# A linear-attention and expert kernel: queries projected transposed, two chunks and half of the heads at a time

## What is computed

```python
q = _heads(x @ wq.T)
k = _heads(x @ wk.T)
v = _heads(x @ wv.T)
# _phi(x, omega):
proj = jnp.einsum('bhnd,md->bhnm', x, omega)
norm = 0.5 * jnp.sum(x * x, axis=-1, keepdims=True)
return jnp.exp(proj - norm) / math.sqrt(M)
# then, with phi_q and phi_k:
kv_cumsum = jnp.cumsum(jnp.einsum('bhnm,bhnd->bhnmd', phi_k, v), axis=2)
out = jnp.einsum('bhnm,bhnmd->bhnd', phi_q, kv_cumsum)
z = 1.0 / (jnp.einsum('bhnm,bhnm->bhn', phi_q, jnp.cumsum(phi_k, axis=2)) + 1e-06)
```

## Time and profile before

| | |
|---|---|
| median of 3 runs | 728.42 us (727.18 to 729.02) |
| the profiled execution: its time, its span | 727.18 us, 725.1 us |
| granted TensorE clock, mean | 0.992 |
| busy share: PE, PEld, DVE, ACT, POOL | 96%, 83%, 74%, 53%, 46% |

### The profile page before, as it was taken

The page is one execution under the profiler, slowest core; times in us unless marked ns, Lnnn a source line. Parts: engine busy times, 40 slices in busy tenths (PEclk is TensorE's granted clock), DMA queues, the critical chain, the costliest instruction groups (busy, mean ns, idle before and its releaser), DMA issues. The chain is left out here.

```text
span 725.1 us, 27349 instructions
## 1 busy us (share of the span) xinstructions
PE 697.4 (96%) x11452; PEld 604.1 (83%) x11452; DVE 536.0 (74%) x1685; ACT 387.6 (53%) x740; POOL 335.6 (46%) x625
## 2 busy tenths in 40 slices
PE   8999999999999999999999999999999789999956
PEld 8788888888888888888888888888887779999942
DVE  6687888878878887888878878888775456565416
ACT  5755566665656665666656566665552144544310
POOL 3002545555544445454545554545447306556550
PEclk9999999999999999999999999999999999999989
DMA  9974000000000000000000000000000154553128
GB/s 252 362 268 178 11 9 11 10 9 11 14 15 10 11 10 11 10 10 11 9 11 11 14 14 9 11 11 11 10 11 14 49 177 130 168 173 113 51 82 304
DMA packets 32705, 47.25 MB, mean 65 GB/s; under 512 B 4132, under 2 KB 20168, under 8 KB 32584
## 3 DMA queue, kind: packets, MB, share of 16 engines
q1 hardware_dynamic: 23296, 32.62, 13.4%
q0 software_dynamic: 4096, 8.42, 3.6%
q10 hardware_dynamic: 5192, 4.47, 1.9%
HBM read 22.21 MB, written 23.36 MB: 63 GB/s over the span
## 5 line engine op out<-in xcount | busy, mean ns | idle before, releaser
L1297 POOL DMA_INDIRECT y_rows<-y_sb,row_id x64 | 62.8, 982 | 66.0 <-DVE y_sb L1442 49.9
L1108 POOL DMA_INDIRECT dispatched<-h_cur,slot x64 | 67.3, 1051 | 17.8 <-issue 16.1
L1376 ACT ACTIVATE hidden<-bank,b_col 128x512 f32<-128x512 f32 x64 | 43.3, 689 | 58.2 <-PE bank L1348 57.8
L632 ACT ACTIVATE phi_k<-expo_k 128x1024 f32<-128x1024 f32 x32 | 33.9, 1058 | 74.5 <-DVE expo_k L768 70.7
L648 ACT COPY v_sb<-bank 128x512 f32<-128x512 f32 x64 | 37.6, 587 | 62.1 <-PE bank L279 58.7
L527 PEld LDWEIGHTS bank<-woT,attT 128*128 128x128 f32 x512 | 61.9, 192 | 3.2 <-ACT attT L738 0.6
L859 DVE TENSOR_TENSOR scores<-bank,within 128x512 f32<-128x512 f32 x64 | 41.2, 686 | 31.2 <-PE bank L310 31.2
L527 PE MATMUL bank<-woT,attT 128*128 128x128 f32 x512 | 62.4, 275 | 0.4 <-ACT attT L738 0.4
L1317 PE MATMUL bank<-w_sb,hidden 128*128 128x128 f32 x512 | 59.7, 275 | 0.8 <-issue 0.8
L137 POOL TENSOR_TENSOR rs<-var,power 128x1 f32<-128x1 f32 x64 | 37.1, 579 | 49.8 <-DVE var L132 49.5
L1317 PEld LDWEIGHTS bank<-w_sb,hidden 128*128 128x128 f32 x512 | 58.3, 192 | 1.2 <-issue 1.2
(11 more groups left out here) (243 smaller groups left out, 2037.9 us busy)
## 6 DMA issues: line engine op xcount, KB each, us to landing
dispatched<-blank SPq DMA_DIRECT2D x16, 524.0 KB, 3.1
region<-dispatched SPq DMA_DIRECT2D x30, 262.0 KB, 2.9
y_rows<-blank SPq DMA_DIRECT2D x8, 512.0 KB, 3.9
w_nat<-in_L_ffn_w_dram SPq DMA_DIRECT2D x8, 256.0 KB, 3.7
y_got<-y_rows SPq DMA_DIRECT2D x8, 256.0 KB, 6.8
y_got<-y_rows ACTq DMA_DIRECT2D x8, 256.0 KB, 7.4
out_dram<-x_sb SPq DMA_DIRECT2D x8, 256.0 KB, 3.7
w_sb<-in_L_ffn_w_dram ACTq DMA_DIRECT2D x6, 256.0 KB, 2.8
```

Source lines behind the costliest of these rows:

```text
L1108: pool.indirect_dma_start(out=dispatched[:, :], in_=h2_cur[par][:], in_offset=None, out_offset=bass.IndirectOffsetOnAxis(ap=slot[par][:, k ...
L1297: pool.indirect_dma_start(out=y_rows[:, :], out_offset=bass.IndirectOffsetOnAxis(ap=row_id[par][:, t:t + 1].bitcast(U32), axis=0), in_=y_s ...
L1376: act.activation(hidden[par][:, k, :], psum[2 + k][:], ACT.Gelu, bias=b1_col[:, bass.ds(e * KH + k, 1)]).then_inc(sem(f"hid{k}_out"), 1)
```

## The change

Of the queries, step c now handles unit n = c + 2. A unit is half of the heads (even or odd n) for the two chunks of a pair. `project_qT` holds 128 columns of `wq` as the stationary operand and streams the 256 tokens of the pair, so that the queries come out transposed: 12 matmuls of 128x256 for a unit. ACT copies them to `qT` (`qT_out`), DVE squares them whole (`square_q`), and `exponent_qT` makes the exponent on PE: omega times q plus a matrix of -0.5 times the squares, 16 f32 matmuls with a 64x64 stationary operand and 256 streamed columns, on the quarters of the array in turn. ACT takes the exponential straight out of PSUM into `phiT_q` (`exps_q`). The weights of pq, the projections q and pq of the old form, the transposes tq and their copies, and DVE's sum and exponents for q are gone. Both feature scales are now one factor on the keys' side. `h` is made four chunks ahead instead of two, with three pairs of buffers. The banks are shared out anew (k and pk in banks 2 and 3, wo behind attT0, rank in bank 7, the first state increment in its own turn), k, v and pk stand next to each other, `wo` before the rank, POOL's scatter ahead of the second normalisation, DVE's `find_places` behind `upd`, and the opening is ordered anew: it now holds two units of queries, the first transposes of the keys, and two more chunks of `h`. The indentation below is cut by 16 columns.

```diff
+h_hi = [tsb(f"h_hi{i}", [P, 2, 2, P], F32R) for i in range(3)]
...
+qT = tsb("qT", [P, HD])
+qT_square = tsb("qT_square", [P, HD])
+omT = tsb("omT", [P, M])
+minus_half = tsb("minus_half", [P, M])
+phiT_q = [tsb(f"phiT_q{i}", [P, NP, 2 * P]) for i in range(2)]
...
-X_PIECES = ((0, 1), (1, 2), (3, 9), (12, 10), (22, 10))
+X_PIECES = ((0, 1), (1, 3), (4, 8), (12, 10), (22, 10))
...
-TURNS = {0: ["q0", "k0", "v0", "pq0", "pk0"], 1: ["q1", "k1", "v1", "pq1", "pk1"],
-         2: ["tk0", "tk1", "a0", "attT0"], 3: ["tq0", "tq1", "a1", "attT1", "rank"],
+TURNS = {0: ["q0", "v0", "pq0"], 1: ["q1", "v1", "pq1"],
+         2: ["tk0", "k0", "pk0", "a0", "attT0", "wo"], 3: ["tk1", "k1", "pk1", "a1", "attT1"],
          4: ["o0", "o2", "h2T", "lg"], 5: ["o1", "o3"],
-         6: ["late0", "hT", "late1"], 7: ["early0", "early1", "wo"]}
+         6: ["hT", "late0", "late1"], 7: ["early0", "early1", "rank"]}
 BANK = {k: b for b, ks in TURNS.items() for k in ks}
-BEFORE = {k: ks[i - 1] for ks in TURNS.values() for i, k in enumerate(ks)}
...
+        def project_qT(n):
+            first = 2 * (n % 2)
+            pair = n // 2
+            hi, lo = h_hi[pair % 3][:, :, 0, :], h_lo[pair % 3][:, :, 0:P]
+            pe.wait_ge(sem("h_split"), 2 * pair + 2)
+            if n == 1:
+                pe.wait_ge(sem("wT_split"), len(WEIGHTS))
+            for side in range(2):
+                if n == 0:
+                    pe.wait_ge(sem(f"v{side}_out"), 1)
+                elif n >= 2:
+                    pe.wait_ge(sem(f"pq{side}_out"), 1 if n == 2 else n)
+                for i in range(2):
+                    o = q_bank(side, n)[:, i * 2 * P:(i + 1) * 2 * P].rearrange("p (c t) -> p c t", t=P)
+                    cols = slice(side * 512 + (first + i) * P, side * 512 + (first + i + 1) * P)
+                    pe.matmul(o, wT_hi["q"][:, cols], hi, start=True, stop=False)
+                    pe.matmul(o, wT_lo["q"][:, cols], hi, start=False, stop=False)
+                    mm = pe.matmul(o, wT_hi["q"][:, cols], lo, start=False, stop=True)
+                mm.then_inc(sem(f"q{side}_in"), 1)
+        def exponent_qT(n, c):
+            if c >= 0:
+                pe.wait_ge(sem("v1_out"), c + 2)
...
+                pe.wait_ge(sem("q_squared"), n + 1)
+            for i in range(2):
+                for w, of in ((omT, queries_of(n)), (minus_half, squares_of(n))):
+                    for side in range(2):
+                        for r in range(2):
+                            cols = slice(side * 512 + i * 2 * P, side * 512 + (i + 1) * 2 * P)
+                            mm = pe.matmul(q_bank(r, n)[half_rows(side), i * 2 * P:(i + 1) * 2 * P],
+                                           w[half_rows(r), :], of[half_rows(r), cols],
+                                           start=(w is omT), stop=(w is minus_half), skip_group_check=True)
+                            if i == 1 and w is minus_half and side == 1:
+                                mm.then_inc(sem(f"pq{r}_in"), 1)
...
+            if c < 0:
                 pe.wait_ge(sem("wT_split"), SPLIT[w] + 2)
+                if w == "k":
+                    pe.wait_ge(sem("h_split"), 1)
+                elif w == "v":
+                    pe.wait_ge(sem(f"k{half}_out"), 1)
+                else:
+                    pe.wait_ge(sem("woT_ready"), 2)
+            elif w == "k":
+                pe.wait_ge(sem(f"tk{half}_out"), c + 1)
+            elif w == "v":
+                pe.wait_ge(sem(f"q{half}_out"), min(c + 3, NCH))
+                if c + 2 >= NCH:
+                    pe.wait_ge(sem(f"pq{half}_out"), NCH)
+            else:
+                pe.wait_ge(sem(f"k{half}_out"), c + 2)
+            bank = psum[BANK[kind]] if w == "v" or w == "pk" else k_bank(half, c)
             cols = slice(half * 512, (half + 1) * 512)
...
+        def features_T(half, c, par):
+            if c >= 2:
+                pe.wait_ge(sem("attT1_out" if half else "wo_out"), c - 1)
+            elif c == 1:
+                pe.wait_ge(sem(f"a{half}_out"), 1)
+            pe.wait_ge(sem("phi_k_ready"), c + 1)
...
+                    pe.wait_ge(sem("pk1_out"), c + 2)
...
-            weights(5)
-            pe.wait_ge(sem("h_split"), 1)
-            project("q0", -1, 0)
-            project("q1", -1, 0)
+            for n in range(2, 6):
+                weights(n)
+            project("k0", -1)
+            project("k1", -1)
+            first_T(1)
+            closing_weights()
+            pe.wait_ge(sem("small_used"), 3)
             weights(6)
             weights(7)
+            project("v0", -1)
+            project("v1", -1)
             modulation(1)
-            project("k0", -1, 0)
-            project("k1", -1, 0)
-            project("v0", -1, 0)
-            project("v1", -1, 0)
-            weights(8)
-            weights(9)
-            first_T(1)
-            project("pq0", -1, 0)
-            project("pq1", -1, 0)
-            closing_weights()
+            first_T(2)
+            project("pk0", -1)
+            project("pk1", -1)
+            first_T(3)
+            project_qT(0)
+            project_qT(1)
             modulation(2)
             modulation(3)
-            project("pk0", -1, 0)
-            project("pk1", -1, 0)
-            bias_T()
+            exponent_qT(0, -1)
+            features_T(1, 0, 0)
+            features_T(0, 0, 0)
+            exponent_qT(1, -1)
...
+            if c:
+                pe.wait_ge(sem("gain1_out"), c)
+            else:
+                pe.wait_ge(sem("mod_used"), 4)
+            if live(c, 4):
+                pe.wait_ge(sem("xn_ready"), c + 5)
+                pe.transpose(psum[BANK["hT"]][:, 0:P], xn[par][:], ident[:]).then_inc(sem("hT_in"), 1)
+            if c:
+                features_T(1, c, par)
+                features_T(0, c, par)
+            if live(c, 2):
+                project_qT(c + 2)
             if front:
-                pe.wait_ge(sem("h_split"), c + 2)
-                project("q0", c, nxt)
-                project("q1", c, nxt)
-            features_T("tq0", c, par)
-            features_T("tk0", c, par)
-            if front:
-                project("k0", c, nxt)
-                project("k1", c, nxt)
-            features_T("tq1", c, par)
-            features_T("tk1", c, par)
+                project("k0", c)
+                project("k1", c)
+                project("v0", c)
+                project("v1", c)
+                project("pk0", c)
+                project("pk1", c)
             if tail:
                 attend_state(1, c - 1, nxt, (j - 1) % CPB)
             state_gain(0, c, par, j)
             if tail:
                 attend(1, c - 1, nxt, (j - 1) % CPB)
-            if front:
-                project("v0", c, nxt)
-                project("v1", c, nxt)
             score(0, c, par)
             score(1, c, par)
+            if live(c, 2):
+                exponent_qT(c + 2, c)
             if last:
                 routing_T(c, par)
-            if live(c, 2):
-                pe.wait_ge(sem("gain0_out"), c + 1)
-                pe.wait_ge(sem("xn_ready"), c + 3)
-                pe.transpose(psum[BANK["hT"]][:, 0:P], xn[par][:], ident[:]).then_inc(sem("hT_in"), 1)
-            if front:
-                project("pq0", c, nxt)
-                project("pq1", c, nxt)
+            if tail:
+                attended_T(0, c)
             if last:
                 routing_logits(c)
             if tail:
-                attended_T(0, c)
                 attended_T(1, c)
-            if c == 0:
-                pe.wait_ge(sem("woT_ready"), 2)
             attend_state(0, c, par, j)
             state_gain(1, c, par, j)
             attend(0, c, par, j)
+            if tail:
+                add_heads(c)
             if last:
                 routing_rank(c)
-            if front:
-                project("pk0", c, nxt)
-                project("pk1", c, nxt)
-            if tail:
-                add_heads(c)
...
+        def qT_out(n):
+            if n >= 2:
+                act.wait_ge(sem("pq1_in"), n)
+            for side in range(2):
+                act.wait_ge(sem(f"q{side}_in"), n + 1)
+                act.copy(queries_of(n)[:, side * 512:(side + 1) * 512], q_bank(side, n)[:]).then_inc(sem(f"q{side}_out"), 1)
...
+        def exps_q(n):
+            pairs = phiT_q[n // 2 % 2][:, n % 2 * 4:n % 2 * 4 + 4, :].rearrange("p (s r) t -> p r s t", r=2)
+            for r in range(2):
+                act.wait_ge(sem(f"pq{r}_in"), n + 1)
+                act.activation(pairs[:, r], q_bank(r, n)[:].rearrange("p (s t) -> p s t", t=2 * P),
+                               ACT.Exp).then_inc(sem(f"pq{r}_out"), 1)
...
+        def square_q(n):
+            dve.wait_ge(sem("q1_out"), n + 1)
+            dve.tensor_tensor(squares_of(n), queries_of(n), queries_of(n), ALU.mult).then_inc(sem("q_squared"), 1)
...
+            if live(c, 5):
+                first_moments(dve, c + 5)
+            if live(c, 2):
```

(22 more changed lines are left out.)

384 lines of the change are left out of this document (186 added, 198 removed).

## The result

The changed kernel takes 730.24 us (median of 13 runs), the old one beside it 727.58: ratio 1.0032, 95% interval 1.0019 to 1.0045. The forecast was 710. So it is slower by a little more than can be told from no change, and 20 us are missing.

A forecast was written before the change was run, and what follows sets the result against it. PE, busy throughout a step, was taken as the bound; -23.2 (29 steps), +3.7 (opening) and +0.6 (end) sum to -18.9 on the profiled 727.18, 708.3; as a median about 709.5, stated as 710, range 702 to 724.

The forecast's parts named there:

- The net of one step, 0.86: PE in one step: 4.12 us of work removed, 3.26 added for projection and exponent, so 0.86 less.
- Rival 2: Exponent's quarter-array matmuls run two at a time, 3.5 us instead of 1.74: about 767; chance 0.12 shared with the weight-load rival.
- rival 3: Weight loads of `wq` show, each 256-column matmul 0.22 us: about 747; chance 0.12 shared with the two-quarters rival.
- Here PE waits 0.07 at once: Heads' first transposes wait for a0_out: 3.0 us after `attend`, while PE has 2.93 of work.
- Rival 1: Handoffs a0_out, wo_out and pk1_out cost more, DVE 0.2 to 0.5 us later each step: 716 to 725; chance 0.18.
- So a steady step costs 16.71 - 0.86 + 0.06 = 15.91. 29 steps: -23.2 us: Steady steps: old step 16.71 us, less 0.86 of PE work, plus 0.06 of waits; 23.2 saved over 29.
- wrong if PE's idle time in a step passes 0.5: Sign that the prediction is wrong: PE idle more than 0.5 us within a step.
- Opening, +3.7: Before step 1: more query units done first and new waits make step 1 start 3.7 us later.
- Step 30, -1.4: Step 30 has no unit of queries, but waits return; about 15.3 us instead of 16.72.
- Step 31, +2.0: Step 31: POOL's `h_cur`, with the scatter in front, comes 2.0 us later for PE.

The follow-up runs named there:

- spread_v: The changed kernel with v's projection moved back between `attend(1)` and the scores: 736.65 us, ratio 1.0142 to the old kernel.

## Why the prediction was wrong

Put piece by piece against the forecast (the profiled execution, us; for the last two pieces the old kernel's 37.3 and 144.8 with what the forecast adds, 2.0 and 0):

```
                                 forecast   measured
start of step 1                    45.4      46.33    +0.9
steps 1 to 29                     461.4     477.44   +16.1
step 30                            15.3      16.96    +1.6
step 31 to the experts             39.3      42.30    +3.0
experts to the end                144.8     144.9     +0.1
```

The ends of these pieces in the changed kernel (the old kernel's first expert transpose is at 580.36, its steps in the earlier trace rows):

```profile
46.33 0.33 PE L635 MATMUL bank<-ident,xn 128*128 128x128 f32 x1
...
523.77 0.31 PE L366 MATMUL bank<-ident,phi_k 128*128 128x128 f32 x1
...
540.73 0.31 PE L366 MATMUL bank<-ident,phi_k 128*128 128x128 f32 x1
...
583.03 0.33 PE L1419 MATMUL bank<-ident,rows 128*128 128x128 f32 x1
```

- **The net of one step, 0.86: right.** 15.89 to 15.91 undisturbed, and both new prices within 0.002 of those taken. Rival 2 (two quarters at a time) and rival 3 (loads that show) are out: 0.217 a group and 0.118 a matmul. The Trainium skill's rule that stood beside rival 2 ("TensorE: Matmul & The Clock Gate", Part 3, The mechanism) doesn't hold for this group: four quarters over 256 columns take 0.217, two to a row group.
- **"Here PE waits 0.07 at once" and the other hand-offs: right or too dear.** 0.2 us of waits for another engine from step 1 to 505 us. Rival 1 is out.
- **"So a steady step costs 16.71 - 0.86 + 0.06 = 15.91. 29 steps: -23.2 us": the step that failed.** It took PE's time to be the sum of its distances between starts. That holds only while instructions come as fast as PE uses them. Stalls at block ends between 48 and 515 us are 14.1 of the 16.1. The other 2 I haven't placed one by one; they lie in the same long steps, as the 17 undisturbed ones average 15.90, and block ends that cost less than 0.3 each add to some 2 us. I had every row for it: 4 us of quarter-array work without a long matmul between, and a stall in the old kernel at 372.72 marked "issue". I looked only for waits on semaphores, and counted instructions by their time, not their number. My line "wrong if PE's idle time in a step passes 0.5" was the right alarm for the wrong reason.
- **Opening, +3.7: short by 0.9.** A stall of 0.43 marked "issue" stands at 46.07 (place 449 + 256*2). Over seven traces with this opening step 1 starts at 45.5 to 48.5, so the rest of the 0.9 is within what one execution differs from another.
- **Step 30, -1.4: the waits were right, what follows them was not.** PE waits 0.69 before k (0.9 forecast) and 1.49 before the heads' transposes (1.7), but then the granted clock falls to 1.2 GHz, and `attend_state`, `state_gain` and `attend` take 2.7 instead of 1.6.
- **Step 31, +2.0: mis-sized.** `h_cur`'s transpose starts 8.45 after the step, in the old kernel 5.44: 3.0 later, not 2.0. I counted the two DMAs (2.4) in front of `h_cur`, but they wait for the slots first (1.49 above), which DVE now finds after the heads' sum. PE itself gets there sooner, so it waits 4.7 against 0.49. From there to the experts it takes 2.0 more than in the old kernel, and PE has half the clock again over 549 to 555 us:

```profile
535.00:540.00 5.00, 5.00 (x114) 4.60 (x113) 2.71 (x14) 1.44 (x5) 1.59 (x5) 0.66 0.02 5
545.00:549.00 4.00, 0.00 (x0) 0.00 (x0) 1.35 (x3) 0.00 (x0) 3.61 (x7) 0.98 0.10 34
549.00:555.00 6.00, 5.82 (x94) 5.40 (x95) 1.84 (x11) 1.70 (x6) 1.63 (x6) 0.50 0.01 3
```

## What to carry to other kernels

Count a stretch's instructions as well as its time: where small matmuls stand together, 256 instructions in about 2 us outran their supply here (14.1 us of stalls), while the same work with a few long ones between, 256 in 3.5 us, seldom did (2.9 us in `spread_v`, 1 in the old kernel). "issue" idle on a busy engine, at places a fixed number of instructions apart, is the mark of it. The cure is not free: an order that spreads the small ones pays for passages and hand-offs (0.5 to 0.7 us a step in two of three orders tried), so move something of the same shape and of middle density, as half the exponent did. Before the last step of a pipeline, look again at every order that was chosen for the steady state; a wait there can cost twice, itself and the clock after it.
